# A perceiver layer on one core: the context's transposes move from TensorE to VectorE, with a second load of the context by feature quarters

## The reference

```python
# x (64, 32, 256), ctx (64, 257, 256), all float32; batches are independent until the last step
x = x + xattn(layernorm(x), ctx)      # 32 queries on 257 keys, per batch
x = x + attn(layernorm(x))            # top 8 of the causal similarities, per batch
x = x + ffn(layernorm(x))             # 8 experts, each token goes to one

# xattn:
Q = x @ Wq + bq;  K = y @ Wk + bk;  V = y @ Wv + bv
K_hat = cos(K @ Wr + br)
out = softmax(Q @ K_hat.T) @ V
# attn:
A = the 8 largest x_t . x_s with s < t
score = (x @ W_q.T) @ (x @ W_k.T).T / sqrt(32), where A, else -1e9
blended = mix * x + (1 - mix) * softmax(score) @ x
out = gelu(blended * gain + bias) * scale
# ffn:
e = argmax(x @ Wr);  out = p_max * (gelu(x @ W1[e] + b1[e]) @ W2[e] + b2[e])
```

## Time and profile before

| | |
|---|---|
| median of 3 runs | 477.11 us (476.13 to 479.04) |
| the profiled execution: its time / its span | 478.89 us / 477.2 us |
| PE busy | 448.3 us, 94% of the span |
| DVE busy | 279.1 us, 58% |
| ACT busy | 259.2 us, 54% |
| POOL busy | 181.0 us, 38% |
| PE's share of the chain that ended last | 85% |
| mean granted clock of TensorE | 0.971 of full speed |

### The profile page before, as it was taken

How to read it: one execution, slowest core, us unless ns; L and a number is a source line. 1 busy time by engine, 2 the same in 40 slices (tenths; PEclk the granted TensorE clock), 3 DMA queues, 4 the chain that set the end, 5 groups by cost and what they waited for, 6 DMA issues and landing times.

```text
span 477.2 us, 10375 instructions
## 1 busy us (share of the span) xinstructions
PE 448.3 (94%) x3249; PEld 327.7 (69%) x3249; DVE 279.1 (58%) x933; ACT 259.2 (54%) x557; POOL 181.0 (38%) x326
## 2 busy tenths in 40 slices
PE   7889999999999999999999889787999999999992
PEld 6645655565555656565656568576999999999991
DVE  2557677879889988898999876554221221222220
ACT  1567577677867876778678555352132232332330
POOL 2830342345254544642553534334133232232110
PEclk9799999999999999999999999978899999999996
DMA  8843521631534326406634552717578556556100
GB/s 215 258 138 100 150 82 58 187 101 43 191 100 148 111 80 188 145 7 227 190 104 132 199 199 83 223 67 265 140 279 289 189 174 226 171 197 232 33 0 1
DMA packets 49337, 70.67 MB, mean 148 GB/s; under 512 B 8446, under 2 KB 38976, under 8 KB 49156
## 3 DMA queue, kind: packets, MB, share of 16 engines
q1 hardware_dynamic: 42820, 59.29, 38.5%
q0 software_dynamic: 3744, 9.46, 5.9%
q10 hardware_dynamic: 2720, 1.26, 1.0%
HBM read 62.37 MB, written 8.53 MB: 149 GB/s over the span
## 4 chain that ended last, share of the span: by engine, by line
PE 85%; DMA 4%; DVE 4%; issue 2%; ACT 2%; POOL 1%; SPq 1%; DVEq 0%; POOLq 0%; ACTq 0%
PE pK L1352 23%; PE pK L1389 17%; PE pT L1375 17%; PE pT L1294 6%; PE b L1294 3%; PE b L1489 3%; PE b L1446 3%; PE b L1511 3%; PE b L1545 3%; DMA stage<-in_ctx_dram 3%; PE b L1476 2%; DMA XF<-in_ctx_dram 2%; PE b L1536 2%; PE pK L1294 1%; PE b L1472 1%
## 5 line engine op out<-in xcount | busy, mean ns | idle before, releaser
L1352 PE MATMUL pK<-stage,Wkr 128*128 128x512 f32 x256 | 123.0, 605 | 0.7 <-ACT stage L1154 0.4
L1180 ACT ACTIVATE XF<-pT,b_now 128x128 f32<-128x128 f32 x184 | 52.2, 368 | 96.4 <-PE pT L1375 96.3
L1389 PE MATMUL pK<-W,XF 128*128 x368 | 88.0, 391 | 5.3 <-DVE XF L805 3.5
L1375 PE MATMUL pT<-XF,stage 128*128 128x128 f32 x736 | 89.1, 280 | 1.9 <-DVE XF L799 1.9
L1375 PEld LDWEIGHTS pT<-XF,stage 128*128 128x128 f32 x736 | 87.6, 195 | 4.2 <-DVE XF L799 2.9
L1389 PEld LDWEIGHTS pK<-W,XF 128*128 128x128 f32 x368 | 69.6, 196 | 15.0 <-issue 6.4
L1352 PEld LDWEIGHTS pK<-stage,Wkr 128*128 128x128 f32 x256 | 44.4, 193 | 38.4 <-issue 37.7
L292 POOL TENSOR_SCALAR ve<-mv 128x1 f32<-128x1 f32 x48 | 12.3, 256 | 141.4 <-DVE mv L600 141.2
L1161 ACT ACTIVATE stage<-pK,bkr 128x512 f32<-128x512 f32 x64 | 42.7, 688 | 29.9 <-PE pK L1352 29.9
L1168 ACT ACTIVATE stage<-stage 128x512 f32<-128x512 f32 x64 | 40.5, 633 | 31.7 <-DVE stage L674 31.7
L674 DVE TENSOR_TENSOR stage<-stage 128x512 f32<-128x512 f32 x64 | 47.4, 741 | 1.2
(11 more groups left out here) (192 smaller groups left out, 671.3 us busy)
## 6 DMA issues: line engine op xcount, KB each, us to landing
stage<-in_L_ffn_W_dram SPq DMA_DIRECT2D x23, 1024.0 KB, 5.0
stage<-in_ctx_dram SPq DMA_DIRECT2D x32, 512.0 KB, 5.1
W<-in_L_ffn_W_dram SPq DMA_DIRECT2D x8, 1024.0 KB, 6.1
rows_by_token<-rows_out SPq DMA_DIRECT2D x16, 256.5 KB
ctx_last<-in_ctx_dram SPq DMA_DIRECT2D x64, 32.0 KB, 4.1
X<-in_x_dram SPq DMA_DIRECT2D x1, 1792.0 KB, 7.9
tokens_by_expert<-no_token POOLq DMA_DIRECT2D x2, 576.0 KB, 4.2
stage<-in_L_ffn_b_dram SPq DMA_DIRECT2D x1, 1024.0 KB, 4.4
```

The source lines that it names most:

```text
L1180: ins = act.activation(f_hT[b][:, n * P:(n + 1) * P], pT[i][:, (n % 4) * P:(n % 4 + 1) * P], ACT.Gelu, bias=b1_now[:, b, n:n + 1])
L1352: mm = pe.matmul(pK[r][:], Wkr[:, c, r * P:(r + 1) * P], ctx_T[:, c, half * 512:(half + 1) * 512], start=c == 0, stop=c == DC - 1)
L1375: mm = pe.matmul(pT[i][:, (n % 4) * P:(n % 4 + 1) * P], W1[q][:, c, n * P:(n + 1) * P], f_inT[:, q % 2, c * P:(c + 1) * P], start=c == 0, ...
L1389: mm = pe.matmul(p_out, f_hT[q % 2][:, n * P:(n + 1) * P], W2[:, bass.ds(e, 1), n, :].rearrange("p o d -> p (o d)"), start=n == 0, stop=n ...
```

## The change

1. The context is loaded a second time, by feature. `quarter_by_feature` puts feature quarter q of a token block on partitions 32q to 32q+31, so that a 32x32 block transpose yields the layout that the projection wants. A DMA moves 256 pieces of 256 B; a half of a group takes 8 DMAs (512 KB), a group 16. There is one buffer `by_feature` for each half, in unused columns of `XF`. It is loaded again when its transpose is done.
2. `ctx_turned`: one DVE `transpose` of 128x1024 float32 in 32x32 blocks for each half, from SBUF to SBUF. PE's `ctx_transposes`, DVE's and ACT's `ctx_T_copy` go. The features in `Wkr` are reordered to match (the copies of `WkT`, the last rows).
3. The PSUM tiles `pT`, now free, hold strips 2 and 3 (`p_turns`).
4. The similarities and the query-key product are one strip of 96 columns (`hqk`, `p_simqk`).
5. `normal_x` moves from DVE to GpSimd, behind `count_pair` and ahead of `add_bv`. GpSimd also makes `hm`, h times the gain, at the end of `self_part`; the message is multiplied with `hm`, and DVE's `mixed` goes: `message` now adds `hg` at once.
6. The copies of xnT, probsT and oT move from DVE to ACT.
7. The router's matmul is split into four strips of 32 tokens.
8. The orders of all lists are new. On DVE, `ctx_turned(s, 1)` stands third in an iteration, ahead of `normal_h`; `out_moments` stands behind the first two strips, ahead of `selected_max` and `ctx_turned(s+1, 0)`.

```diff
...
+        by_feature = [XF[:, 4 * D + i * 4 * D:4 * D + (i + 1) * 4 * D] for i in range(2)]
...
-        ctx_T = room(DC * BG * CF).rearrange("p (c n) -> p c n", c=DC)
+        ctx_T_flat = [room(DC * 512) for _ in range(2)]
+        ctx_T = [t.rearrange("p (n c t) -> p c n t", c=DC, t=T) for t in ctx_T_flat]
...
+        p_turns = [pK[0][:], pK[1][:], pT[0][:], pT[1][:]]
...
+        def quarter_by_feature(g, half, j, q):
+
+            return (by_feature[half][q * T:(q + 1) * T, j * 2 * D:(j + 1) * 2 * D].rearrange("p (n f) -> p n f", f=2 * T),
+                    c_in[BG * g + 2 * half + j, 0:CF, q * 2 * T:(q + 1) * 2 * T].rearrange("(n i) f -> i n f", i=T))
...
+            def normal_x(g):
+                pool.wait_ge(S["rs1_r"], g + 1)
+                at_least(pool, S["xnT_tr"], g - 1)
+                pool.tensor_scalar(xn[:, g % 2, :], group_of(X, g), mv1[:, 0:1], rs1[:, 0:1], ALU.subtract, ALU.mult
+                                   ).then_inc(S["xn_r"], 1)
...
+                at_least(pool, S["msg_mm"], g - 1)
+                pool.tensor_tensor(hm[:, g % 2, :], h[:, g % 2, :], gain_msg[:], ALU.mult).then_inc(S["hm_r"], 1)
...
                 if s + 1 < NG:
+                    normal_x(s + 1)
                     add_bv(s + 1)
...
+            def load_by_feature(g, half, quarters=range(P // T)):
+                for j in range(2):
+                    for q in quarters:
+                        sp.dma_start(*quarter_by_feature(g, half, j, q)).then_inc(by_feature_ld[half], 16)
...
+            load_by_feature(0, 0, (0, 1))
+            load_by_feature(0, 1)
...
+            sp.wait_ge(S["ctxT_r"], 1)
+            load_by_feature(1, 0)
             load_ctx(0, 0)
-            sp.dma_start(last_rows, c_in[:, CF, :]).then_inc(S["last_ld"], 16)
             load_ctx(1, 1)
...
-            for g in range(2, NG):
-                next_group(g, g % 2)
-                if g % 2:
+            for g in range(1, NG):
+                sp.wait_ge(S["ctxT_r"], 2 * g)
+                load_by_feature(g, 1)
+                if g >= 2:
+                    next_group(g, g % 2)
+                if g + 1 < NG:
+                    sp.wait_ge(S["ctxT_r"], 2 * g + 1)
+                    load_by_feature(g + 1, 0)
...
+            def ctx_turned(g, half):
+
+                v.wait_ge(by_feature_ld[half], 16 * 2 * (P // T) * (g + 1))
+                at_least(v, S["kproj"], 4 * (g - 1) + 2 * half + 2)
+                v.transpose(ctx_T_flat[half], by_feature[half]).then_inc(S["ctxT_r"], 1)
...
             def message(g):
                 v.wait_ge(S["msg_mm"], g + 1)
-                v.tensor_tensor(y_msg[:], p_msg, gain_msg[:], ALU.mult).then_inc(S["ymsg_r"], 1)
+                v.wait_ge(S["hg_r"], g + 1)
+                at_least(v, S["gelu_r"], g)
+                v.tensor_tensor(y[:], p_msg, hg[:, g % 2, :], ALU.add).then_inc(S["y_r"], 1)
...
             for s in range(NG):
-                ctx_T_copy(s, 0)
                 if s >= 2:
                     residual_stats(s - 2)
-                xnT_copy(s)
-                if s >= 2:
                     residual_moments(s - 2)
-                if s >= 4:
-                    mixed(s - 4)
                 if s >= 1:
-                    score_max(s - 1)
+                    ctx_turned(s, 1)
                 if s >= 2:
                     normal_h(s - 2)
...
                 if s >= 4:
                     out_moments(s - 4)
...
+                    selected_max(s - 2)
+                if s + 1 < NG:
+                    ctx_turned(s + 1, 0)
...
+            def ctx_project(g, half, r):
+                u = 2 * half + r
+                if g == 0:
+                    pe.wait_ge(S["wkr_cp"], 1)
+                pe.wait_ge(S["ctxT_r"], 2 * g + half + 1)
+                at_least(pe, S["turns_r"], 4 * (g - 1) + u + 1)
+                for c in range(DC):
+                    mm = pe.matmul(p_turns[u], Wkr[:, c, r * P:(r + 1) * P], ctx_T[half][:, c],
                                    start=c == 0, stop=c == DC - 1)
...
-                        own = hT[:, c, j * T:(j + 1) * T]
-                        mm = pe.matmul(p_sim[j * T:(j + 1) * T, :], own, own, start=c == 0, stop=c == DC - 1,
-                                       skip_group_check=True)
+                        mm = pe.matmul(p_simqk[j * T:(j + 1) * T, :], hqk[:, c, j, 0:T], hqk[:, c, j, :],
+                                       start=c == 0, stop=c == DC - 1, skip_group_check=True)
                 mm.then_inc(S["sim_mm"], 1)
-                for c in range(DC):
-                    mm = pe.matmul(p_qk, hT[:, c, :], WqkT[:, c, :], start=c == 0, stop=c == DC - 1)
-                mm.then_inc(S["qk_mm"], 1)
...
```

More of the change, by code:

```diff
@@ L636, in _ @@
             v.wait_ge(S["lastT_tr"], 1)
             v.tensor_copy(last_T.rearrange("p c n -> p (c n)"), b7[:, 0:DC * B]).then_inc(S["lastT_cp"], 1)
-            normal_x(0, 0)
-            v.wait_ge(S["lastK_mm"], 1)
-            v.wait_ge(S["bkr_cp"], 1)
-            for r in range(DC):
-                v.tensor_scalar(last_turns[:, r, :], b6[:, r * B:(r + 1) * B], bkr[:, r:r + 1], None, ALU.add
-                                ).then_inc(S["last_turn"], 1)
-            v.wait_ge(S["last_turn"], 2)
@@ L962, in _ @@
                 if s + 1 < NG:
+                    v.wait_ge(S["xn_r"], s + 1)
                     moments(s + 1, st1, mv1, "st1_r", "mv1_r")
                 if s >= 1:
-                    inverse_sumA(s - 1)
+                    score_max(s - 1)
+                if s >= 3:
+                    weights_T(s - 3)
+                whole(s, 0)
+                if s >= 1:
+                    inverse_sumA(s - 1)
+                fraction(s, 0)
+                if s == 0:
+                    last_turned()
+                    small_copies()
+                    scalars()
                 if s >= 6:
@@ L1054, in _ @@
             normal_h(15)
-            mixed(13)
             begin(1)
@@ L1160, in turn @@
                 at_least(act, S["frac_r"], 4 * g + u - 1)
-                act.activation(turns[r], pK[r][:], ACT.Identity, bias=bkr[:, r:r + 1]).then_inc(S["turns_r"], 1)
+                act.activation(turns[r], p_turns[u], ACT.Identity, bias=bkr[:, r:r + 1]).then_inc(S["turns_r"], 1)
             def sine(g, b, u):
@@ L1171, in _, with xnT_copy, probsT_copy, oT_copy @@
             act.wait_ge(S["bkr_cp"], 1)
+            def xnT_copy(g):
+                act.wait_ge(S["xnT_tr"], g + 1)
+                at_least(act, S["qproj"], g)
+                act.copy(xnT[:].rearrange("p c n -> p (c n)"), p_xnT).then_inc(S["xnT_cp"], 1)
+            def probsT_copy(g):
+                act.wait_ge(S["pT_tr"], g + 1)
+                at_least(act, S["pv"], g)
+                act.copy(probsT[:].rearrange("p c n -> p (c n)"), p_pT).then_inc(S["pT_cp"], 1)
+            def oT_copy(g):
+                act.wait_ge(S["oT_tr"], g + 1)
+                at_least(act, S["aproj"], g)
+                act.copy(o_T[:].rearrange("p c n -> p (c n)"), p_oT).then_inc(S["oT_cp"], 1)
             def gelus(j, q, i):
@@ L1550, in router @@
                 for c in range(DC):
-                    mm = pe.matmul(p_route, xn3T[:, c, :], Wroute[:, c, :], start=c == 0, stop=c == DC - 1)
+                    for j in range(BG):
+                        own = slice(j * T, (j + 1) * T)
+                        mm = pe.matmul(p_route[own, :], xn3T[:, c, own], Wroute[:, c, :],
+                                       start=c == 0, stop=c == DC - 1, skip_group_check=True)
                 mm.then_inc(S["route_mm"], 1)
             for s in range(NG):
-                ctx_transposes(s, s % 2, s // 2, 0)
+                if s == 0:
+                    last_transposes()
                 xn_T(s)
+                ctx_project(s, 0, 0)
+                if s == 0:
+                    last_project()
                 if s >= 1:
```

327 lines of the change are left out of this document (143 added, 184 removed).

## The result

The changed kernel takes 481.62 us (median of 14 runs, 479.15 to 484.74), the kernel before, run beside it, 478.49 (14 runs, 476.04 to 479.47). The ratio is 1.0075, 95% interval 1.005 to 1.010: a little slower. Predicted were 468 us and a gain of 2%. The profiled execution of the changed kernel took 479.15 us, its span 477.3, which is level with before's (478.89 and 477.2). But it is the fastest of its 14 executions, with the highest granted clock of them (0.959; the others have 0.944 to 0.959), and before's lies above the median of its own. So the traces show where things went, and not the 3.1 us between the medians.

A forecast was written before the change was run, and what follows sets the result against it. PE was taken to bound the loop at 16.08 us an iteration: 21.8 us gained there, less 10.4 for POOL, 1.5 at the start and 1 behind the loop, makes 8.9, so 470.0, as median 468 us; range 453 to 483.

The forecast's parts named there:

- the sum's first two terms: Loop: 13 iterations from 3 to 15 at 14.4 us in place of 16.08 gain 21.8 us; POOL loses 10.4.
- the price of the wait: Starts of iterations 8, 10, 12 and 14: DVE stands still 3.0 us, costing 2.6 us each, 10.4 in all.
- the base iteration: Loop without POOL's wait: 14.4 us per iteration, between 14.0 and 15.0, from DVE 14.0, PE 13.9 and 0.4 for meetings.
- The stretch on POOL: GpSimd's unbroken list from rstd_out to last_key in odd iterations: grows from 8.0 to 9.3 us by normal_x 0.56 and hm 0.79.
- if the clock fell in the gaps: Named, without a size, as something that would make the sum wrong, beside a transpose over 2 us.
- rival 3: DVE and POOL slow each other more: up to 1.35 us an iteration, 17.5 us in all, 486 us; chance 0.13.
- The tail: Behind the loop: 1 us lost, where a scatter stands ahead of a deviation once more, with hm ahead of it.
- The transposes on DVE: Two 128x1024 transposes per iteration on DVE: 1.28 us each, between 0.75 and 3.95.
- The strided moving operand: Projection on PE reading its moving operand in runs of 32 elements: cost 0, at most 0.5 us per iteration, no gain.
- rival 1: By-feature loads make DMA the limit: above 32 ns per piece it decides; at 45 ns, 17.8 us an iteration, 500; chance 0.1.
- The start: Iteration 1: DVE stands still until about 35 us for group 1's second half by feature; a loss of 1.5 us.
- Rival 2: POOL's stretch between layer norms doesn't bind DVE: 20.3 us gained, 457 us; chance 0.22.

The follow-up runs named there:

- experiment 7: Changed kernel with GpSimd's normal_x multiplying twice in place of subtracting and multiplying: 478.43 us, ratio 1.002.
- kernel of 5: Changed kernel with GpSimd's scatters moved to the next even iteration and group 1's second half by feature loaded earlier: 463.28 us, ratio 0.971.
- experiment 1: Changed kernel with GpSimd's scatters moved from the end of odd iterations to the next even one, behind last_value: 467.34 us, ratio 0.978.
- experiments 5 and 6: Changed kernel with later scatters and the other load order at the start: 463.28 us; the same with normal_x back on VectorE: 462.82 us.
- experiment 11: Kernel of 5 with x's transposes and ScalarE's copy later (462.54 us), plus first expert block's gather ahead of rstd_out(11): 454.27 us, ratio 0.951.
- experiment 10: Kernel before with scatters one iteration later: 479.16 us, ratio 1.002; separately, with the changed kernel's orders behind the loop: 472.86 us, ratio 0.992.

## Why the prediction was wrong

The step that failed is the sum's first two terms, "13 iterations from 3 to 15 x (16.08 - 14.4) = 21.8 us gained; 10.4 lost to POOL". The mechanism was right in its place and even in its size: a wait for `rs` at the starts of iterations 8, 10, 12 and 14 and of no others (above 0.24 us), foretold as 3.0 us, measured as 3.08, 2.95, 2.94 and 2.26. What failed is the size of these two terms, the price of the wait and the base iteration, with stalls of iterations 14 and 15 that the sum put at nothing: it has 11.4 us of gain for iterations 3 to 15, where the ledger has 7.6 of loss. Of these 19.0 us the price of the wait is 5.4 (iterations 8, 10 and 12), the base 5.6 (without 14 and 15), iteration 14 4.1 and iteration 15 5.0, less 1.1 for before, whose iterations 3 to 14 took that much more than 16.08 each. That the time came within the stated range is luck: the tail gave 9.6 us more than foretold. Point by point:

- **The stretch on POOL.** `normal_x` was priced as a form like line 404's, 0.56 us; it takes 1.24 (experiment 7). Line 404's two products don't stand for a subtraction and a product; the shape was the same, the operations weren't. The stretch became 9.9 us, not 9.3; DVE asked 6.7 us after its start, not 6.0, so the wait stayed 3.1. The Trainium skill (GPSIMD Engine Reference, Performance versus the Vector engine) has GpSimd 1.96 times as slow as VectorE in an elementwise addition of two tensors. No run here has that operation on both engines; for `normal_x`, 1.24 us on GpSimd stand against 0.41 on VectorE, three times, and the two products' 0.56 are 1.4 times that 0.41.
- **The price of the wait.** I took 3.0 us of waiting for 2.6 us of time. Iterations 8, 10 and 12 take 19.1 us; the even ones of the kernel of 5, which has no such stall, take 14.7, so the wait cost 4.4 us each, 1.8 more than foretold. PE's granted clock fell from 1.00 to 0.91 in these windows, and its work in iteration 8 took 1.7 us longer than in the same iteration of experiment 1 (15.77 against 14.08). The prediction named it among the things that would make the sum wrong ("if the clock fell in the gaps") and gave it no price.
- **The base iteration.** 14.4 was taken within 14.0 to 15.0; the eight iterations without a stall take 119.9 us in all, 15.0 each, 4.7 us more than eight times 14.4 (1.4 of them in iteration 13); the three stalled ones have 0.3 each on top, by the 14.7 of the kernel of 5. DVE has 13.7 us of work, not 13.3: beside a busier GpSimd, its two strip operations take 547 and 792 ns on the mean in the loop, where before had 464 and 746 in the same view; four of each make 0.5 us. That is rival 3's mechanism at a third of its price. Single operations show beside what. DVE, then GpSimd, in the changed kernel's iteration 8:

```profile
150.97 0.43 DVE L715 TENSOR_SCALAR stage<-stage 128x512 f32<-128x512 f32 x1 [0.66 <-ACT stage L1172]
...
152.04 0.95 DVE L715 TENSOR_SCALAR stage<-stage 128x512 f32<-128x512 f32 x1
```
```profile
150.42 1.24 POOL L312 TENSOR_SCALAR xn<-X,mv,rs 128x256 f32<-128x256 f32 x1
151.74 0.97 POOL L318 TENSOR_TENSOR X<-X,bv 128x256 f32<-128x256 f32 x1
152.68 0.90 POOL L433 TENSOR_TENSOR hg<-h,gain_self 128x256 f32<-128x256 f32 x1
```

  Beside `normal_x` the strip's rounding takes 0.43 us, beside the two operations with two inputs 0.95. This fits experiments 5 and 6, in which moving `normal_x` leaves the means as they are; the new operation of the slow kind is `hm`, which no experiment took away. The Trainium skill (SBUF — State Buffer, Who interferes with whom) names two kinds of VectorE instruction that contend with GpSimd: those with two SBUF inputs, when GpSimd reads SBUF, and copies and `tensor_scalar` when they run in a mode that takes both ports. The subtraction is of the first kind and the rounding, a `tensor_scalar`, can be of the second. That both are slower agrees with it; why the rounding is not slower beside `normal_x`, no run here shows.
- **Iterations 14 and 15.** 14 takes 21.1 us, 4.1 over the forecast: `plan_rows` and `plan_used` stand in DVE's list ahead of the last strips and of y, and PE waits 2.90 us for y. They stood there in before too, whose iteration 14 took 16.35 us (237.08 to 253.43): its PE had work of its own for as long, and hid them. In 15, PE waits 4.12 us for rows that it had in time before. GpSimd's timeline, before and then after:

```profile
260.28 0.22 POOL L292 TENSOR_SCALAR ve<-mv 128x1 f32<-128x1 f32 x1 [2.48 <-DVE mv L600]
...
263.16 1.53 POOL L376 DMA_INDIRECT f_row<-rows_by_token,token_i  x1 [0.17 <-issue]
```
```profile
269.19 0.22 POOL L305 TENSOR_SCALAR ve<-mv 128x1 f32<-128x1 f32 x1 [4.65 <-DVE mv L640]
...
272.72 1.37 POOL L396 DMA_INDIRECT f_row<-rows_by_token,token_i  x1 [0.17 <-issue]
```

  The gather starts 13.9 us into the iteration in place of 9.7. Most of this comes from DVE: it asks for the deviation of `rstd_out(11)`, behind which `gather(0)` stands, 10.4 us in, not 6.9. `hm` ahead of the gather adds 0.9. I had looked at no stall of the last two iterations; experiment 11 shows what such a wait is worth.
- **The tail.** Foretold as 1 us lost, it gave 8.6 back. The orders behind the loop were in the diff (`rstd_out` ahead of the gathers), and I priced only the scatter ahead of one deviation, instead of reading which waits of before ended there. Without this gain the changed kernel would have been some 4 us slower still (experiment 10).
- **What was right.** The transposes on DVE: 1231 ns (1.28 foretold). The joined strip: 0.47 us (0.45). The strided moving operand: a strip takes 1.88 us, and no gain or loss. DMA: share 0.79 of 15.14 us is 12.0 us, less the 6.3 of before it is 22 ns a piece (20 foretold), and no wait for it behind iteration 1: rival 1 falls. The start: DVE waited until 35.66 (35 foretold), for 1.1 us lost (1.5). Rival 2 falls by the 12.2 us of waits. Rival 3 holds in part, as said above.

## What to carry to other kernels

An engine with half its time idle can still have no room at one place of its list: before adding to it, measure the unbroken stretch up to the instruction that somebody waits for, and move what nobody waits for (here two indirect DMAs) out of it. Price a wait of TensorE above its length, for what follows it runs slower for a while. Price an operation on GpSimd by a row with the same arithmetic and the same company on VectorE, not only the same shape; and read the tail of a changed order as closely as the loop, where a few moved lines were worth 4.4 us.

## What the runs showed of the hardware

- On GpSimd, a 128x256 float32 operation with two scalars per partition takes 0.56 us as two products and 1.24 us as a subtraction and a product, in the same place of the same list; the two products of `o_norm` took 0.56 us in before and 0.56 to 1.09 us in the changed kernel.
- TensorE's granted clock was 0.91 in iterations with one wait of 3.1 to 3.2 us and 1.00 in those from 3 to 13 whose waits stayed below 1.3 us. It was 0.60 over the 3.6 us behind the wait of 3.22 us, where a strip took 3.17 us in place of 1.88, and 0.58 over the 3.7 us behind the wait of 4.12 us at the end of the loop. Taking away a wait of 4.7 us there gave 6.4 us.
- VectorE's transpose of 128x1024 float32 in 32x32 blocks takes 1.23 us, 1.2 ns a column.
